# A graph layer on one core: sums of squares of the node update kept in PSUM, and the logarithm taken in two operations

## What is computed

```
h = relu(layernorm(x))
em = relu(layer_norm(concat(h[src], h[dst]) @ msg_w + msg_b)) * edge_weight
messages = segment_sum(em, dst) / count
combined = concat(h, messages)
h_new = relu(layer_norm(combined @ upd_w + upd_b))
gate = sigmoid(h @ gate_w + gate_b)
out = x + gate * h_new + (1 - gate) * h
```

## Time and profile before

| what | value |
|---|---|
| median of 3 runs | 932.8 us (932.32 to 932.9) |
| span of the profiled execution | 994.9 us, mean granted clock 0.695 |
| DVE busy in it | 896.4 us, 90% |
| ACT busy in it | 881.3 us, 89% |
| POOL busy | 672.5 us, 68% |
| PE busy | 711.9 us, 72% |
| node stage, steady part | from about 50 to about 495 us |

### The profile page before, as it was taken

How to read it: one execution, slowest core, us unless ns; L and a number is a source line. 1 busy time by engine, 2 the same in 40 slices (tenths; PEclk the granted TensorE clock), 3 DMA queues, 4 the chain that set the end, 5 groups by cost and what they waited for, 6 DMA issues and landing times.

```text
span 994.9 us, 19018 instructions
## 1 busy us (share of the span) xinstructions
PE 711.9 (72%) x3696; PEld 556.2 (56%) x3696; DVE 896.4 (90%) x3914; ACT 881.3 (89%) x3758; POOL 672.5 (68%) x602
## 2 busy tenths in 40 slices
PE   2477778777777777777756767787778787777861
PEld 1355556555555555555545656666656666666651
DVE  7499999999999999999997489999989999999984
ACT  3499999998999899989987689999999999999973
POOL 4677878777666667677757357677666776665466
PEclk9655555555555555555567789899889889998995
DMA  4244544455545555555423112233311211111110
GB/s 142 54 125 157 160 145 156 152 164 155 159 153 166 156 157 156 164 158 156 135 75 93 45 56 92 80 95 97 97 63 53 66 64 65 61 54 57 53 70 33
DMA packets 60147, 107.94 MB, mean 108 GB/s; under 512 B 14278, under 2 KB 16150, under 8 KB 60082
## 3 DMA queue, kind: packets, MB, share of 16 engines
q1 hardware_dynamic: 39756, 71.88, 20.8%
q0 software_dynamic: 18912, 34.84, 13.5%
q10 hardware_dynamic: 1414, 0.53, 0.2%
HBM read 56.01 MB, written 55.12 MB: 112 GB/s over the span
## 4 chain that ended last, share of the span: by engine, by line
ACT 60%; PE 13%; issue 11%; DVE 6%; another core or an unknown queue 6%; POOL 3%; ACTq 1%; DMA 1%; DVEq 0%; POOLq 0%
ACT hrow L392 16%; ACT junk L399 16%; ACT work L426 10%; ACT xload L392 4%; PE pt L1177 3%; ACT rs L379 3%; PE pm L1229 3%; ACT lnv L374 3%; POOL out L596 3%; PE pm L1231 3%; ACT work L1102 2%; PE py L1248 2%; ACT at L1045 2%; ACT work L1045 2%
## 5 line engine op out<-in xcount | busy, mean ns | idle before, releaser
L596 POOL DMA_INDIRECT out<-work,sidx x196 | 209.4, 1069 | 124.4 <-issue 55.6
L591 POOL DMA_INDIRECT ring<-in_x,src_i x196 | 220.0, 1123 | 90.5 <-issue 57.3
L1177 PE MATMUL pt<-ident,hrow 128*128 128x128 f32 x588 | 147.4, 399 | 142.6 <-ACT hrow L392 119.5
L426 ACT ACTIVATE work<-work,gt 128x128 f32<-128x128 f32 x589 | 205.1, 426 | 4.2 <-issue 3.0
L1211 PE MATMUL py<-w_u,work 128*128 128x129 f32 x784 | 204.5, 442 | 0.0
L1211 PEld LDWEIGHTS py<-w_u,work 128*128 128x128 f32 x784 | 175.6, 329 | 40.8 <-issue 40.8
L1177 PEld LDWEIGHTS pt<-ident,hrow 128*128 128x128 f32 x588 | 99.0, 202 | 175.6 <-ACT hrow L392 146.0
L591 POOL DMA_INDIRECT ring<-in_x,gidx x140 | 156.9, 1121 | 53.7 <-issue 42.2
L399 ACT ACTIVATE junk<-py 128x128 bf16<-128x128 f32 x588 | 155.4, 293 | 29.9 <-remote 29.8
L392 ACT ACTIVATE hrow<-xload,nb,rs 128x128 f32<-128x128 f32 x392 | 163.5, 514 | 3.0 <-DVE nb L385 2.7
L458 DVE SCALAR_TENSOR_TENSOR work<-py,rs,g_upd 128x128 f32<-128x128 f32 x588 | 163.2, 338 | 0.0
(11 more groups left out here) (163 smaller groups left out, 1506.7 us busy)
## 6 DMA issues: line engine op xcount, KB each, us to landing
xload<-in_x SPq DMA_DIRECT2D x98, 256.0 KB
out<-work SPq DMA_DIRECT2D x98, 256.0 KB
running_sums<-acc SPq DMA_DIRECT2D x49, 256.0 KB
staged_target_rows<-work SPq DMA_DIRECT2D x14, 256.0 KB
ring<-staged_target_rows SPq DMA_DIRECT2D x14, 256.0 KB
ring<-in_x,src_i POOLq DMA_INDIRECT x196
out<-work,sidx POOLq DMA_INDIRECT x196
ring<-in_x,gidx POOLq DMA_INDIRECT x140
```

The lines of the kernel that those rows point to most:

```text
L426: last = nc.scalar.activation(t_buf[:, g.at % 4, k, :], t_buf[:, g.at % 4, k, :], ACT.Relu, scale=gt[:, g.at % 4, k:k + 1])
L591: pool.indirect_dma_start(out=dest, out_offset=None, in_=rows, in_offset=bass.IndirectOffsetOnAxis(ap=idx, axis=0), **(if_tail if rows is ...
L596: pool.indirect_dma_start(out=out, out_offset=bass.IndirectOffsetOnAxis(ap=idx, axis=0), in_=rows, in_offset=None, **if_tail).then_inc(s, 16)
L1177: last = nc.tensor.transpose(dest[:, k * H:(k + 1) * H], rows[:, k, :], ident[:, :])
```

## The change

A new `node_squares` takes the place of `squares` for node groups: the four sums go to four columns of `pa` in PSUM (slot * 4 + k) and no longer to `mv`. A new `logs_node` takes the place of `logs` with 8 columns: one Ln over 4 columns of `mv`, one Ln over 4 columns of `pa` (of `mv` in the first 4 steps, when there are no sums yet). Both write to `lnv`, and the second one raises the semaphore that `rstds` waits for. Groups of the edge stage are as before.

```diff
+        def logs_node(act, s):
+            c = s.at % 4
+            nc.scalar.activation(lnv[:, c, 0:G], mv[:, c, 0:G, 1], ACT.Ln, bias=eps_col[:, :])
+            squares_of = pa[:, c * G:c * G + G] if live(s.back(4), NG) else mv[:, c, G:2 * G, 1]
+            one_mark(nd["ln"], act, s, nc.scalar.activation(lnv[:, c, G:2 * G], squares_of, ACT.Ln, bias=eps_col[:, :]))
...
+        def node_squares(prod, slot):
+            for k in range(G):
+                nc.scalar.activation(junk[:, 0, k, :], prod[:, k, 0:H], ACT.Square, scale=float(H) ** -0.5,
+                                     accum_out=pa[:, slot * G + k:slot * G + k + 1])
...
         def post(act, d, g, slot, at, n=G, scale=float(H) ** -0.5):
             d["upd"].after(act, g)
-            squares(py[:, g.at % 2], slot, at, n, 0, scale)
+            if d is nd:
+                node_squares(py[:, g.at % 2], slot)
+            else:
+                squares(py[:, g.at % 2], slot, at, n, 0, scale)
...
-                logs(act, nd, s, 2 * G)
+                logs_node(act, s)
                 filling = not beyond(s, 4)
...
-                    logs(act, nd, node, 2 * G)
+                    logs_node(act, node)
                     rstds(act, nd, node, 2 * G)
```

## The result

| | time, us | ratio to before |
|---|---|---|
| before | 932.83 (932.32 to 932.9) | |
| changed | 938.35 (936.55 to 939.13) | 1.0056 (1.0041 to 1.007) |

The change costs 5.5 us. I had forecast 7.6 (940.4 us), slower with 0.60. The profiled execution of the changed kernel spans 937.3 us, 1.8 less than its time as a run.

A forecast was written before the change was run, and what follows sets the result against it. DVE was taken to bound the node step at 4.60 us, with ACT 0.07 below; the second Ln's 0.143 makes ACT's step 4.674, adding 7.0 us plus 0.6 at the seam to 932.8: 940.4 us, range 930.3 to 946.8.

The forecast's parts named there:

- DVE set the step at 4.60 us with 0.07 on ACT to spare, and ACT takes over: Node stage: DVE sets the step before; ACT's grows to 4.674 us, 0.074 beyond DVE's; likeliest case, chance 0.50.
- The second Ln costs 0.143 us: ACT's logarithm: one Ln of 8 goes, two of 4 come, net +0.143 us a step, 0.19 at most.
- Four reads into PSUM save nothing: ACT's four accumulator reads a node step: no saving taken from writing to PSUM, 0.37 us a step at best.
- my bound of nothing: Lower bound on the four reads' saving: a read costs the same into PSUM as into SBUF.
- ACT's own step of 4.531: Node stage before the change: ACT's instructions, added up from start to next start, come to 4.531 us a step.
- The sum: ACT's node step 4.531 + 0.143 = 4.674 us; over 94 steps 7.0 us, plus 0.6 at the seam: +7.6 us.
- 0.6 at the seam: Four seam steps, where the Exp follows the Ln directly, each grow by 0.143 us or a little more: 0.6 us.
- The waits of the profile: ACT idle ahead of the squares 20 times, 40.9 us; if in timed runs, the addition costs 14.0 us, giving 946.8.
- Rival 1: Reads into PSUM get cheap, 0.04 us saved each, DVE still sets the step: 932.8 us, down to 930.3; chance 0.30.
- Rivals 2 and 3: 2: reads nearly free, 921 to 929 us, 0.10; 3: PSUM Ln as dear as SBUF's, 945 or 951 us, 0.10.
- What I said would show it: ACT's read to next square: 0.09 forecast, 0.05 rival 1, below 0.03 rival 2; DVE's L437 4.67 apart, idle before it.

The follow-up runs named there:

- split_only2: Changed kernel with sums in SBUF and both Lns of 4 columns out of SBUF, second timing: 944.92 us beside 932.83 for the kernel before, ratio 1.0128.
- before_less_dve2: Kernel before, with one row of four left out of DVE's last addition, second timing: 927.08 us beside 932.83, ratio 0.9936.
- the experiment with one Ln: Changed kernel with one Ln of 8 columns out of SBUF, and one row of four left out of DVE's last addition: 923.58 us beside 933.36, ratio 0.9893.
- both_psum: Changed kernel with the squares of rows 0 to 2 also in PSUM, row 3's in SBUF, DVE's full work: 933.59 us beside 933.36, ratio 1.0003.
- junk_psum_less_dve: Kernel before with squares written to PSUM, sums in SBUF, one row of four left out of DVE's last addition: 938.91 us beside 933.36, ratio 1.0062.
- both_first_less_dve: Changed kernel with squares of rows 1 to 3 in PSUM, row 0's in SBUF, DVE's last addition one row short: 928.15 us beside 932.83, ratio 0.9957.

## Why the prediction was right, and where it was off

**DVE set the step at 4.60 us with 0.07 on ACT to spare, and ACT takes over.** Right. With less work on DVE the kernel before gains 5.75 us, and the changed one keeps its step of 4.652.

**The second Ln costs 0.143 us.** Right. Out of SBUF it adds 4.732 - 4.548 = 0.184 us a step (split_only2 against before_less_dve2, ACT the bound in both), and out of PSUM an Ln takes 0.147 rather than 0.188 to the next start: 0.143. The element count hardly entered.

**Four reads into PSUM save nothing.** This term was mis-sized, and its reasoning was wrong. I argued that a write's destination takes no time, since the Square and `ge` write to SBUF at 0.05. A read into PSUM does take 0.047 less. What I couldn't have from the rows is that the square behind it then takes 0.04 more. The net saving is 0.048 us a step in the experiment with one Ln, 0.039 in the changed kernel: near to my bound of nothing, but from two larger terms that I had both left out (0.182 won, 0.128 lost back), so that this term came out near is luck. The Trainium skill's page "ScalarE: Activation LUTs" ("Step-by-step: what each stage is for") has PSUM as the faster destination. The trace agrees for the single read: at the seam, where ACT isn't behind, it lasts 0.15 us in the profile of the changed kernel, against 0.20 in the kernel before at the same place. It doesn't agree for a whole row: a square of 128 in a run of writes to PSUM takes 0.157 to the next start (both_psum), no less than into SBUF, and squares that alternate with SBUF made the step 4.663 rather than 4.548 (junk_psum_less_dve against before_less_dve2).

At the seam, after the change:

```profile
477.25 0.15 ACT L413 ACTIVATION_READ_ACCUMULATOR junk<-py 128x1 f32 x1
477.31 0.30 ACT L413 ACTIVATE junk<-py 128x128 bf16<-128x128 f32 x1
```

and before:

```profile
509.16 0.20 ACT L399 ACTIVATION_READ_ACCUMULATOR junk<-py 128x1 f32 x1
509.25 0.27 ACT L399 ACTIVATE junk<-py 128x128 bf16<-128x128 f32 x1
```

The square behind the read is 0.03 longer there as well, so the surcharge doesn't need a full engine.

**ACT's own step of 4.531.** Off by 0.017: that was measured while ACT caught up with DVE. When ACT is what all wait for, the same instructions take 4.548. The ReLU and the Ln behind the sums take 0.298 and 0.207 rather than 0.292 and 0.192.

**The sum.** 4.548 + 0.143 = 4.691, less the step of 4.652, leaves 0.039 for the sums in PSUM; I had 4.531 + 0.143 = 4.674. The step grew by 0.052 rather than 0.074 us: times 94, 4.9 us, and my forecast's 0.6 at the seam make 5.5. Measured 5.5. Of the 0.6 the traces show only that the Lns of one seam step take 0.47 us rather than 0.32 to the Exp's start (471.79 to 472.26 after, 503.85 to 504.17 before). No run isolates it in the time: both_psum has the same Lns there and still takes the time of the kernel before within about 0.1%. The gap to my 7.6 is the 0.022 a step.

**The waits of the profile.** Rightly kept out of the sum: ahead of the node squares they aren't in the changed kernel's profile nor, but for two, in the second one of before. Rival 1 needed a saving of 0.019 us a read; a read and what it does to the next instruction gave 0.039 / 4 = 0.010. With PSUM for most squares too it is (4.691 - 4.591) / 4 = 0.025, and both_psum comes out at no change, as that rival said. Rivals 2 and 3 didn't happen.

**What I said would show it** held in part. The read at 0.05 would by my list have meant rival 1: I looked at one instruction where the pair was the least unit to look at. The idle time ahead of DVE's first operation isn't there, since DVE's wait lies between `omg` and `nb`, under a long row.

## What to carry to other kernels

Where two engines are within 2% of each other, add up starts rather than durations for each, and find whose lead grows: that gave the step, its slack of 0.07 us and the sign of this change. An ACT instruction of 4 columns costs nearly what one of 8 does (0.188 and 0.192 us), so a change that splits one into two has to win back a whole instruction elsewhere. Price a change of destination on the run of instructions behind it, since the time that one row gives back may stand in the next, or a few rows later.

## What the hardware showed that I had not expected

- Where all four squares of a step went to one memory and their sums to the other, a Square took about 0.04 us more, in either direction (0.195 to 0.202 against 0.157; with sums in PSUM all but the step's first). In both_psum only the first square did, at the turn into PSUM; in both_first_less_dve, where that square goes to SBUF, none did. A single square into SBUF between two reads into PSUM (row 3 of both_psum) took 0.157 as well. In both, a later ReLU grew instead. So the price goes with the pattern of writes, and no rule for a single row came out of these runs. A ReLU with two operands by partition shows no such surcharge (0.385).
- A read of the accumulator takes 0.093 us to the next start with its result in SBUF (0.088 behind a square into PSUM) and 0.046 to 0.051 with it in PSUM. A square of 128 takes 0.157 with either, where nothing alternates.
- With ACT as the bound its rows grow longer without taking more of the engine: a ReLU into `hrow` lasts 633 ns in before_less_dve2, where four in a row lasted 1.67 us in all (0.51 for the last), both at 0.385 to the next start. There a duration isn't what the instruction costs; that it tells how far the engine is behind is my reading, not tested.

```profile
L392 ACT ACTIVATE hrow<-xload,nb,rs 128x128 f32<-128x128 f32 x308 | 137.6, 633 | 0.0
```

- The same kernel took 933 us on two chips and 975 on another, with a node step of 4.600 us on the slow one and, where DVE sets it on a quiet one (both_psum), 4.598. What that chip loses its time to, and what the unnamed waits ahead of the squares are, I haven't settled.
